# Gated cross-attention on one Trainium2 core: K first in the step, single scores interleaved with halves of K and V, values in one block, row DMAs on ScalarE's queue

## The reference, cut to what matters

```python
def xattn(query, key, value):            # key = value = ctx, (16, 361, 256); query = layernorm(x), (16, 100, 256)
    Q = query @ Wq.T + bq;  K = key @ Wk.T + bk;  V = value @ Wv.T + bv      # split in 16 heads
    dot = einsum('bhsd,bhtd->bhst', Q, K) / sqrt(16)
    out = einsum('bhst,bhtd->bhsd', softmax(dot), V)
    return out.reshape(B, 100, 256) @ Wh.T + bh

x = x + tanh(g_xattn) * xattn(layernorm(x), ctx, ctx)
x = x + tanh(g_ffn) * ffn(layernorm(x))  # rms norm, gate over 8 experts, top 2, low-rank changes of w1, w3, w2
```

## Time and profile before

| | us |
|---|---|
| median of 3 runs | 538.91 |
| lowest and highest | 536.33, 541.66 |
| the profiled execution | 538.21 |
| its span in the trace | 536.4 |

### The profile page before, as it was taken

How to read it: one execution, slowest core, us unless ns; L and a number is a source line. 1 busy time by engine, 2 the same in 40 slices (tenths; PEclk the granted TensorE clock), 3 DMA queues, 4 the chain that set the end, 5 groups by cost and what they waited for, 6 DMA issues and landing times.

```text
span 536.4 us, 11868 instructions
## 1 busy us (share of the span) xinstructions
PE 512.6 (96%) x4392; PEld 465.6 (87%) x4392; DVE 351.5 (66%) x774; ACT 259.4 (48%) x578; POOL 293.3 (55%) x339
## 2 busy tenths in 40 slices
PE   8879899999899999999998999999999999999995
PEld 6658698888788888788788999999999999999993
DVE  5857577777677777787756777765476555754443
ACT  4457446555455555556757523353335333343331
POOL 6474446665455456552549964844367433944441
PEclk9999999999999999999989989999999999999998
DMA  6774766776676777765111000000000100001000
GB/s 213 194 229 130 193 175 152 180 179 156 138 172 164 175 174 188 162 140 114 19 17 17 0 1 2 1 1 31 2 2 0 32 1 0 2 0 32 1 0 31
DMA packets 50888, 45.83 MB, mean 85 GB/s; under 512 B 33967, under 2 KB 40275, under 8 KB 50832
## 3 DMA queue, kind: packets, MB, share of 16 engines
q1 hardware_dynamic: 40782, 20.92, 16.9%
q0 software_dynamic: 6704, 15.93, 12.4%
q10 hardware_dynamic: 3346, 8.23, 5.3%
HBM read 20.59 MB, written 6.66 MB: 51 GB/s over the span
## 4 chain that ended last, share of the span: by engine, by line
PE 81%; DMA 8%; DVE 6%; ACT 3%; issue 2%; POOL 1%; SPq 0%; POOLq 0%; DVEq 0%; ACTq 0%
PE bank L1315 13%; PE bank L1177 9%; PE bank L1194 7%; PE bank L1207 7%; PE bank L1367 6%; PE bank L1319 6%; PE bank L1332 6%; DMA QS<-crow 6%; PE bank L1160 5%; PE bank L1347 4%; PE bank L1152 3%; PE bank L1240 2%; PE bank L1350 2%; DMA xs<-x 2%; PE bank L1281 2%
## 5 line engine op out<-in xcount | busy, mean ns | idle before, releaser
L922 DVE TENSOR_REDUCE nmax<-bank 100x1 f32<-100x361 f32 x256 | 128.1, 527 | 56.1 <-PE bank L1177 52.8
L408 POOL TENSOR_TENSOR awl<-hb,awh 128x400 fp32r<-128x400 f32 x64 | 71.9, 1125 | 101.6 <-ACT awh L616 101.6
L517 ACT ACTIVATE pt<-bank 120x400 f32<-120x400 f32 (+1 forms) x192 | 82.7, 504 | 26.1 <-PE bank L1194 25.8
L1177 PE MATMUL bank<-KS,QS 96*100 96x362 f32 x256 | 89.8, 385 | 4.4 <-DVE nmax L922 3.9
L616 ACT ACTIVATE awh<-hb 128x400 fp32r<-128x400 f32 x64 | 34.5, 539 | 118.4 <-DVE hb L868 118.2
L861 DVE TENSOR_TENSOR hb<-sil,bank 128x400 f32<-128x400 f32 x64 | 36.5, 570 | 83.7 <-PE bank L1332 39.4
L344 POOL DMA_DIRECT2D KS<-kn x64 | 32.6, 517 | 96.9 <-PE bank L1177 52.7
L1177 PEld LDWEIGHTS bank<-KS,QS 96*100 96x100 f32 x256 | 42.1, 166 | 24.0 <-issue 12.9
L1194 PE MATMUL bank<-QS,KS 97*120 97x200 f32 (+1 forms) x384 | 51.4, 270 | 4.4 <-DMA QS<-crow 3.8
L1194 PEld LDWEIGHTS bank<-QS,KS 97*120 97x120 f32 (+1 forms) x384 | 49.0, 185 | 6.8 <-DMA QS<-crow 6.1
L868 DVE TENSOR_TENSOR hb<-hb,wbT 128x400 f32<-128x400 f32 x64 | 46.0, 718 | 2.1
(11 more groups left out here) (185 smaller groups left out, 1134.0 us busy)
## 6 DMA issues: line engine op xcount, KB each, us to landing
KS<-kn SPq DMA_DIRECT2D x128, 90.5 KB, 2.9
KS<-kn POOLq DMA_DIRECT2D x64, 90.5 KB, 2.8
craw<-ctxT POOLq DMA_DIRECT2D x14, 361.0 KB, 6.5
QS<-q_dram POOLq DMA_DIRECT2D x92, 50.0 KB, 5.3
q_dram<-qn ACTq DMA_DIRECT2D x4, 400.0 KB, 5.6
o_dram<-on SPq DMA_DIRECT2D x16, 100.0 KB
xr<-o_dram SPq DMA_DIRECT2D x16, 100.0 KB
y<-xs SPq DMA_DIRECT2D x16, 100.0 KB
```

The lines of the kernel that those rows point to most:

```text
L408: nc.gpsimd.tensor_tensor(awl[:, g % 2, slot], hb[:, slot], awh[:, g % 2, slot].bitcast(F32), ALU.subtract).then_inc(m["p_awl"], 1)
L517: nc.scalar.activation(pt[0:TW[t], u % 6, :], pT[u % 3][0:TW[t], 0:CS], ACT.Exp, scale=float(DH) ** -0.5).then_inc(m["act_e"], 1)
L922: nc.vector.tensor_reduce(nmax[:, pos:pos + 1], pS[h % 2][0:S, 0:T], AX.X, ALU.max, negate=True).then_inc(m["dve_s"], 1)
L1177: mm(pS[h % 2][0:S, 0:TP], QS[b % 3][0:96, g, h % 2, j, :], KS[b % 3][0:96, g, j, :], start=True, stop=True).then_inc(m["pe_s"], 1)
```

## The change

- On PE, `row_turn(i, 1)` opens the step. K comes next, in halves of three matmuls (`k_part`) with one head between each two; V follows in the same way (`v_part`). The values of batch i are no longer done in groups of 12 matmuls (three units) through this step and the next, but all 12 units at the end of step i. In the last step (i = 15), which has no heads, they stay in groups.
- `pt` gets 12 places for 6, one per unit.
- The DMA of the row goes from SP's queue to ACT's: it is issued behind the copy, once the copy has ended.
- The late weights go from ACT's queue to POOL's, behind `ctx_low`.
- ACT: `row_out(i, 1)` first; both `k_high` before `v_out(b, 0)`, which moves behind the exponentials 3 to 5; `v_out(b, 1)` before `row_out(i+1, 0)`.
- DVE: `k_low` behind head 2 and head 4 (before: 4 and 7); `root` behind head 15.

```diff
-        pt = sba("pt", [121, 6, CS])
+        pt = sba("pt", [121, UN, CS])
...
-            def row_store(b, half):
-                sp.dma_start(QS[b % 3][96:97, 2 * half:2 * half + 2, :, :, :].rearrange("o a b c d -> o (a b c d)").bitcast(F32),
-                             crow[:, half, :].bitcast(F32)).then_inc(m[("cr_a", "cr_b")[half]], 16)
...
@@ gpsimd, behind ctx_low
+                if 0 <= i - 3 < len(late):
+                    late_load(i - 3)
...
@@ scalar, row_out
                 nc.scalar.activation(crow[:, half, :], row_bank(b, half)[0:H // 2, 0:S], ACT.Copy).then_inc(m["act_c"], 1)
+                act.wait_ge(m["act_c"], 2 * b + half + 1)
+                act.dma_start(QS[b % 3][96:97, 2 * half:2 * half + 2, :, :, :].rearrange("o a b c d -> o (a b c d)").bitcast(F32),
+                              crow[:, half, :].bitcast(F32)).then_inc(m[("cr_a", "cr_b")[half]], 16)
...
-                wait(act, "pe_pv", n - 5)
-                nc.scalar.activation(pt[0:TW[t], u % 6, :], pT[u % 3][0:TW[t], 0:CS], ACT.Exp,
+                wait(act, "pe_pv", n - UN + 1)
+                nc.scalar.activation(pt[0:TW[t], u, :], pT[u % 3][0:TW[t], 0:CS], ACT.Exp,
...
@@ tensor
+            def k_part(b, j, p0, p1):
+                for p in range(p0, p1):
+                    (hw, hc), k = TERMS[p // KT], p % KT
+                    last = mm(pP[(1, 0)[j]][:, 0:TP], wkv[:, 0, hw, k, j * 128:(j + 1) * 128],
+                              cth[:, b % 2, hc, k, :], start=p == 0, stop=p == 5)
+                if p1 == 6:
+                    last.then_inc(m["pe_k"], 1)
...
@@ tensor, body
+                wait(pe, "act_v", min(NT * (i + 2), NT * B))
+                wait(pe, "act_c", 2 * i)
+                row_turn(i, 1)
+                st_unit(i, 0)
+                st_unit(i, 1)
+                st_unit(i, 2)
...
+                    k_part(b, 0, 0, 3)
+                if has_s(i):
+                    s_head(i + 1, 1)
+                if has_k(i):
+                    k_part(b, 0, 3, 6)
...
                     s_head(i + 1, 15)
+                    pv_unit(i, 0)
...
+                    pv_unit(i, 11)
```

More of the change, by code:

```diff
@@ L651, in body @@
                 if has_k(i):
-                    k_high(b, 1)
+                    wait(act, "pe_pv", i * UN)
+                    v_out(b, 0)
                 if i == B - 2:
@@ L983, in body @@
                     head(i + 1, 1)
-                if i in (11, 12):
-                    root(0, 7 * (i - 11))
+                    head(i + 1, 2)
+                if has_k(i):
+                    k_low(b, 0)
                 if has_s(i):
-                    head(i + 1, 2)
                     head(i + 1, 3)
-                if i in (11, 12):
-                    root(0, 7 * (i - 11) + 1)
-                if has_s(i):
                     head(i + 1, 4)
                 if has_k(i):
-                    k_low(b, 0)
+                    k_low(b, 1)
                 if has_s(i):
@@ L1036, in body @@
                 if has_s(i):
-                    head(i + 1, 12)
                     head(i + 1, 13)
-                if i in (11, 12):
-                    root(0, 7 * (i - 11) + 5)
+                    head(i + 1, 14)
                 if i == 1:
@@ L1050, in body @@
                     variance(i - 3)
+                if has_s(i):
+                    head(i + 1, 15)
+                if i in (11, 12):
+                    for k in range(7 * (i - 11), 7 * (i - 11) + 6):
+                        root(0, k)
                 if i == 11:
                     root(0, 6)
-                if has_s(i):
-                    head(i + 1, 14)
-                    head(i + 1, 15)
             for i in range(0, B):
@@ L1149, in k_proj, with v_part @@
                     pe.wait_ge(m["ctx_l"], b + 1)
[L1150 to L1154, removed]
+                k_part(b, j, 0, 6)
+            def k_part(b, j, p0, p1):
[5 more added lines that the diff above has]
+                    last.then_inc(m["pe_k"], 1)
             def v_proj(b, t):
+                v_part(b, t, 0, 6)
+            def v_part(b, t, p0, p1):
                 bank = (pS[0], pS[1], pT[2])[t] if b == 0 else pP[1] if b == 1 and t == 1 else pP[0]
[L1158 to L1162, removed]
+                for p in range(p0, p1):
+                    (hw, hc), k = TERMS[p // KT], p % KT
+                    last = mm(bank[0:TW[t], 0:D], cth[:, b % 2, hc, k, T0[t]:T0[t] + TW[t]],
+                              wkv[:, 1, hw, k, :], start=p == 0, stop=p == 5)
+                if p1 == 6:
+                    last.then_inc(m["pe_v"], 1)
             def s_head(b, h):
@@ L1509, in body @@
                 if has_s(i):
-                    s_head(i + 1, 8)
+                    s_head(i + 1, 9)
+                if has_k(i):
+                    wait(pe, "act_v", NT * b + 1)
+                    v_part(b, 1, 0, 3)
+                if has_s(i):
+                    s_head(i + 1, 10)
+                if has_k(i):
+                    v_part(b, 1, 3, 6)
+                if has_s(i):
                     if has_o(i):
@@ L1515, in body @@
                     row_turn(i + 1, 0)
[L1516 to L1521 removed]
+                    s_head(i + 1, 11)
                 if i == B - 2:
```

142 lines of the change are left out of this document (60 added, 82 removed).

## The result

The changed kernel takes 530.59 us at the median of 11 runs (527.83 to 537.56), the kernel before 534.35 in 11 runs of the same series. The ratio is 0.9899, 95% interval 0.9866 to 0.9932: faster by 1.0%, some 5 us. The medians are of all runs; every ratio here leaves out runs that are over 1.5% above the fastest of the same kernel. Forecast were 526.2 us and a range of 518 to 538. The direction and the time inside the range are right.

A forecast was written before the change was run, and what follows sets the result against it. PE was taken to set the step, with DVE next and deciding how much gain is kept. 13 steps from 197.9 to 185.9 us, first and last steps nothing net: 538.2 - 12.0 = 526.2 us, range 518 to 538.

The forecast's parts named there:

- The walk: One step followed from its opening row transpose through PE, DVE and ACT, with DVE pacing heads: 14.3 us a step.
- the block of values: 48 value matmuls in one piece at the step's end: 2.56 us, three passages into values and three out saved, 0.5.
- The price of the DMA's issue on ACT: Issuing the row's DMA on ACT, taken as 0.67 us ahead of K's high part, lengthens the step by 0.3 us.
- The floor of 13.7: PE alone, without waiting for DVE, would need 14.6 - 0.5 - 0.3 - 0.1 = 13.7 us a step.
- The row's DMA: On ACT's queue the row lands in about 4 us, with 6.1 us of room in each half; then nothing waits.
- Rival A: The row still lands late in a third of steps, losing 2 us and clock: 8.5 us back, 534.7; chance 0.12.
- The first step: Its row transpose waits for head 15 of batch 0, +0.4 us, against about -0.4 inside that step.
- Last steps: 0: The last steps, taken as having no K and V, neither gain nor lose time: 0.
- The sum: 13 steps from 197.9 to 185.9 us, -12.0; taken from the profiled 538.2 this gives 526.2 us.
- B: PE alone is the bound: 13.7 us a step, 19.8 us saved, 518.4 us; chance 0.14.
- C: DVE starves and becomes the bound, idling over 2.0 us outside the value block: 15.6 a step, 543 us; chance 0.12.
- D: ACT's queue blocks longer than 0.67 us, or passages in cut K and V cost more: 14.9 a step, 534; chance 0.12.

The follow-up runs named there:

- experiment 2: The changed kernel with the row's DMA back on SyncE's queue, everything else as changed; ratio to the kernel before 0.9916, median 533.15 us.
- experiment 3: The kernel before with only the row's DMA issued by ACT, order on PE as before; ratio to the kernel before 0.9957.
- experiment 4: The changed kernel with values in four groups again: in all steps, ratio to the kernel before 1.0208; only in the step i = 14, ratio 0.9891.

## Why the prediction was right, and where it was not

**The step.** The mechanism was right, and the match of the number is luck. The walk has no stalls, so its 14.3 is to be held against an undisturbed step, 14.05. Its stations hold within 0.2: K's low part at 3.5, the second row transpose at 8.46, y at 10.74, head 15 at 11.41, the row transpose waiting for nothing, roots hidden (the steps with them take 14.08). What it missed is the block of values: 2.56 was put, 2.20 was measured. The prediction could have had most of that, since its four groups of 0.64 hold three passages more than the block, 0.2 by its own price. The average came to 14.34 because stalls of 0.27 a step, which the forecast put at nothing, filled the gap. The price of the DMA's issue on ACT was given as 0.3; it is 0.57 (experiment 2). That error is not in the 14.3, as the walk includes the issue; it is in the 14.0 that the walk gave without it, where 13.48 was measured. The floor of 13.7 also takes off 0.1 that no item of the sum names.

**The row's DMA.** This term failed. "I take about 4, nearer the latter, as ACT's queue is otherwise empty. Then nothing waits." The landing is still 6.4 to 6.9 us in six steps, for a room of 6.1, and the weight loads wait 3.0 us. Rival A named it, with 0.65 a step; the steps average 0.27 above the undisturbed 14.07. The move to ACT's queue did help in the old order (experiment 3), where it took away nearly all waits, by the ring or by SyncE's time. In the new order it helps less. There the row competes with a larger backlog: KS loads are issued until 0.7 us before the row transpose (135.47 to 142.46 for one at 143.19), all behind the store of `on`, where they ended 2.2 us before it in the old order (158.43 to 162.12 for one at 164.37). The run with the late weights at the end shows that 512 KB less are enough to clear it. The Trainium skill, "DMA: Bandwidth & Descriptors", in its section "Issuing engines are not separate DMA queues", says that transfers from different engines share the same 16 engines; the trace agrees for the new order (share 0.88 to 1.08 from 187 to 191 us, and the row lands behind that). By that the prediction had the landing stay at 5.4 to 7 us, and so it did. The same section of the Trainium skill says that only issue time is saved. Experiment 3 does not contradict it: there the waits of the weight loads went from 6.1 and 4.1 us to 1.2, and SyncE's saved issue time of 0.67 us a row can be the reason.

**The edges.** The first step was right: the extra wait and the gain inside it cancel (its successor opens at 56.80, before at 56.74). "Last steps: 0" was wrong by 0.8: the step with heads but without K and V takes 13.4. Before, it took 12.6. PE is busy 11.6 us of it in both kernels, and the weight loads wait 2.9 us for reductions instead of 1.6. That the values no longer fill these gaps is not the cause shown: with groups in that step alone it took 14.3 (experiment 4). The cause stays open.

**The sum.** It was made between a profiled execution of 538.21 and a model without stalls. The runs say -1.0%, the sum said -2.2%, and the pair of traces -1.9%. In the traces the terms add up: 11.5 us in the 13 steps, 0.8 back at the end, 0.1 at the start, and 0.2 behind the loop. The other 5 us lie between the profiled executions and the rest, on both sides. The prediction took 538.21 for typical, by three runs; the median of 11 is 534.35 (in the three later series 536.7 to 538.4). And the changed kernel's other executions run at lower granted clocks than its profiled one. That waits of 1 to 2 us with half clock behind them make the difference is argued and not shown: such waits stand in traces of the kernel before and of experiments, not in the two of the changed kernel, where the longest is 0.9. Rivals B, C and D did not occur: in the undisturbed step DVE idles 1.3 us outside the block (14.05 less 10.89 of work and the wait of 1.90), under the 2.0 of C, and the weight loads' waits for reductions are 10 us in 15 steps, 0.7 a step, just under the 0.8 that I had named as the point of being wrong.

## What to carry to other kernels

When a step is rearranged, ask of each block what it hides, not only what it costs: the values in one piece were worth more as cover for VectorE's last reduction than as saved passages. Moving a small urgent DMA to another engine has three prices that must be read apart: the issue time on the new engine and what stands behind it (0.57 us a step here), the issue time that the old engine gets back for its other loads, and the backlog of all DMA engines, with which the landing of the small one went here on either queue. And a gain read from two single executions is not to be trusted before timed runs: here it was 10.4 us for some 5.

## What was not expected of the hardware

The block of 48 value matmuls costs 46 ns a matmul (2.20 us) where groups of 12 cost 53 (0.64 us); by the prediction's price of 0.07 to 0.09 a passage, most of that is one passage for four. The length of a wait does not tell whether the clock falls. In the run with the late weights at the end it fell to 0.57 for 4 us (219 to 223) behind a wait of 1.58 us and stayed at 1.00 behind one of 1.66; in the kernel before it fell to 0.60 behind the wait of 2.01 and stayed at 1.00 behind one of 1.92 (140.57, clock of 140.6 to 144.6). Behind the 0.78 at 135.79 in the changed kernel it stayed at 1.00 too. What decides it stays open. That KS stacks could be issued ahead of the store of the outputs on SyncE's queue, which would spread the backlog, follows from the timelines (K is ready at 4 us in the step, SyncE issues at 7); it was not tried.
